# Row maxima of the attention scores as sixteen more rows of the query stack

## What is computed

```python
def reference(x, w_qkv, b_qkv, w_out, b_out, w12, w3, gate_w):
    xn = _layernorm(x, axis=-1)
    return x + attention(xn, ...) + experts(xn, ...)

# attention: 16 heads of 16 features, windows of 128 tokens every 64 tokens
    scores = jnp.einsum('bhnqd,bhnkd->bhnqk', qw, kw) / jnp.sqrt(jnp.float32(D))
    probs = jax.nn.softmax(scores, axis=-1)
    ow = jnp.einsum('bhnqk,bhnkd->bhnqd', probs, vw)
# experts: the best 2 of 8 for each token, softmax of their gate scores as weights
    h12 = jnp.einsum('btd,ehd->bteh', x, w12)
    hidden = jax.nn.silu(h1) * h2
    expert_out = jnp.einsum('bteh,edh->bted', hidden, w3)
```

## Time and profile before

| what | value |
|---|---|
| median of 3 runs | 773.25 us (772.63 to 775.06) |
| the profiled execution | 772.46 us |
| its span in the profile | 770.3 us |
| PE busy | 709.6 us (92%) |
| DVE busy | 579.9 us (75%) |
| ACT busy | 416.8 us (54%) |
| POOL busy | 318.0 us (41%) |

### The profile page before, as it was taken

One profiled execution on the slowest core, in us unless ns is written; L12 is line 12 of the kernel. 1 busy time (PEld: TensorE's weight loads), 2 busy tenths in 40 slices (PEclk: granted clock), 3 DMA queues, 4 the chain that ended last, 5 costly groups with the idle time before them and its releaser, 6 DMA issues.

```text
span 770.3 us, 18229 instructions
## 1 busy us (share of the span) xinstructions
PE 709.6 (92%) x6144; PEld 570.6 (74%) x6145; DVE 579.9 (75%) x975; ACT 416.8 (54%) x769; POOL 318.0 (41%) x360
## 2 busy tenths in 40 slices
PE   0997788797999999999999999999989999999995
PEld 0986566685888778887888778878868787877784
DVE  4953897976787777777777777778758869797884
ACT  0221133235667667676676676766734555655653
POOL 4000369211435445444454444444411235566653
PEclk9975799998999999999999999999999999999999
DMA  8898083472111111111111111111136677875830
GB/s 280 303 327 231 27 221 117 116 240 89 49 48 48 48 54 48 48 49 52 49 51 44 53 49 48 54 44 49 49 101 192 199 230 203 253 206 174 220 116 29
DMA packets 66179, 92.61 MB, mean 120 GB/s; under 512 B 6257, under 2 KB 53233, under 8 KB 66129
## 3 DMA queue, kind: packets, MB, share of 16 engines
q1 hardware_dynamic: 56096, 65.68, 28.5%
q0 software_dynamic: 6864, 18.75, 7.7%
q10 hardware_dynamic: 3168, 7.48, 2.8%
HBM read 59.06 MB, written 32.83 MB: 119 GB/s over the span
## 4 chain that ended last, share of the span: by engine, by line
PE 79%; DVE 11%; DMA 3%; issue 3%; ACT 2%; POOL 1%; SPq 1%; DVEq 0%; ACTq 0%; POOLq 0%
PE PS L1143 71%; PE PS L1370 4%; DVE SMALL L839 3%; DVE XN L1010 2%; PE PS L1348 2%; DMA XN<-in_x 2%; PE PS L1166 1%; DVE WALL L833 1%; PE PS L1226 1%; DMA xt_scratch<-WALL 1%; POOL XN L575 1%; ACT WORK L673 1%; DVE WORK L912 1%; SPq L371 1%; DVE WORK L919 0%
## 5 line engine op out<-in xcount | busy, mean ns | idle before, releaser
L333 DVE TENSOR_TENSOR WS<-WALL,WS 128x1024 fp32r<-128x1024 f32 x144 | 176.5, 1226 | 86.8 <-ACT WS L765 82.8
L1143 PE MATMUL PS<-WS,XTS 128*128 128x512 f32 x852 | 234.3, 411 | 2.1 <-DVE XTS L833 1.6
L1143 PEld LDWEIGHTS PS<-WS,XTS 128*128 128x128 f32 x852 | 151.0, 190 | 46.3 <-DVE XTS L833 13.3
L765 ACT ACTIVATE WS<-WALL 128x1024 fp32r x144 | 152.2, 1058 | 38.3 <-issue 35.8
L1143 PE MATMUL PS<-WALL,WORK 128*128 x568 | 136.3, 383 | 0.8 <-ACT WORK L781 0.8
L1143 PEld LDWEIGHTS PS<-WALL,WORK 128*128 128x128 f32 x568 | 102.2, 190 | 13.1 <-issue 1.0
L616 POOL DMA_INDIRECT WORK<-xn_scratch,WORK x72 | 98.3, 1366 | 23.8 <-issue 21.6
L707 ACT ACTIVATE WORK<-PS 128x512 f32<-128x512 f32 x128 | 69.8, 595 | 63.9 <-PE PS L1143 61.1
L620 POOL DMA_INDIRECT ys_scratch<-SIDE,WORK x36 | 41.6, 1156 | 115.5 <-ACT SIDE L791 115.5
L583 POOL TENSOR_TENSOR OTS<-SIDE,XN 128x256 f32<-128x256 f32 x32 | 23.8, 745 | 147.6 <-DVE XN L1010 99.6
L839 DVE TENSOR_REDUCE SMALL<-PS 128x8 f32<-128x1024 f32 x64 | 77.7, 1214 | 8.9 <-PE PS L1143 8.9
(11 more groups left out here) (125 smaller groups left out, 1082.6 us busy)
## 6 DMA issues: line engine op xcount, KB each, us to landing
WALL<-ys_scratch SPq DMA_DIRECT2D x16, 512.0 KB, 6.8
parts_scratch<-WORK SPq DMA_DIRECT2D x32, 240.0 KB, 2.6
QS<-parts_scratch SPq DMA_DIRECT2D x16, 480.0 KB, 4.4
WALL<-in_wexp ACTq DMA_DIRECT2D x16, 384.0 KB
WALL<-in_wexp SPq DMA_DIRECT2D x16, 384.0 KB
XN<-in_x SPq DMA_DIRECT2D x4, 1024.0 KB, 12.8
xn_scratch<-XN SPq DMA_DIRECT2D x4, 1024.0 KB, 6.9
WALL<-in_x SPq DMA_DIRECT2D x8, 512.0 KB, 5.7
```

Source lines behind the costliest of these rows:

```text
L333: eng.tensor_tensor(out=WS[:, 1 - k, half, 1], in0=weights, in1=WS[:, 1 - k, half, 0].bitcast(F32), op=ALU.subtract).then_inc(low_ready[ha ...
L765: act.activation(WS[:, 1 - k, half, 0], weights, ACT.Copy).then_inc(high_ready[half], 1)
L1143: return pe.matmul(o, a, b, start=start, stop=stop)
```

## The change

The negated maxima are no longer added by a matmul of their own. `KS` gets 16 more rows (`DEEP` = 112). They are constant: in row `96 + 8 * part + i` stand ones for every head whose number modulo 8 is `i`, and zeros elsewhere. `QS`'s buffer already has 128 partitions; its rows 96 to 111 now get the negated maxima, for all eight heads of the unit side by side, on the window's 128 columns. One matmul over 112 rows then gives the shifted scores. The copy out of `T_BANK` moves from DVE (`take_negm`, 16 x 128 elements) to ACT (`take_shift`, line 711 of the changed file, 16 x 1024 elements), where it is the first instruction of a step, ahead of `take_part` or `take_values`. `SEL` and `NEGM` go. `EJ` gets a buffer of its own, with the same readers. `CONSTS` falls from 22 to 18 (one fill and two selects of `SEL`, one fill of `NEGM`), and POOL makes the constant rows behind them: one fill and two selects over 16 x 10240 bf16 elements. PE waits for these before its first `scores`.

```diff
@@ -61,6 +61,7 @@
 STK = NLEV * HD
+DEEP = STK + 2 * HH
 BLOCKS = (0, 2, 1, 3)
@@ -119,8 +120,8 @@
         QS = QALL[0:STK]
-        EJ = QALL[STK:STK + 1, 0, 0, 0:2 * XS_TILES].bitcast(I32)
-        KS = sb("KS", [STK, 2, H, SPAN], BF16)
+        KS = sb("KS", [DEEP, 2, H, SPAN], BF16)
+        EJ = sb("EJ", [1, XS_TILES], I32)[:]
 
@@ -130,14 +131,12 @@
         IDB = IDF[:].bitcast(BF16).rearrange("p (n k) -> p n k", k=2)[:, :, 1]
-        SEL = sb("SEL", [STK, HH, P], BF16)
         SIDE = sb("SIDE", [P, D])
...
         UNIT = sb("UNIT", [P, 3 * HD])
-        NEGM = sb("NEGM", [STK, 2, P], BF16)
         PW = sb("PW", [P, 2, NT])
@@ -246,6 +245,7 @@
 
+        SHIFT_ROW = T_BANK[STK:DEEP, 0:P // 2].bitcast(BF16)
         TOK_BANK = (bank(5), bank(6))
@@ -319,7 +319,7 @@
 
-        CONSTS = 22
+        CONSTS = 18
 
@@ -505,10 +505,6 @@
                                    pattern=[[-1, P]], channel_multiplier=1))
-            one(pool.memset(SEL[:], 0.0))
-            for part in range(2):
-                one(pool.affine_select(out=SEL[:], in_=SEL[:], compare_op=ALU.not_equal, fill=1.0, base=-HH * part,
-                                       pattern=[[-1, HH], [0, P]], channel_multiplier=1))
             one(pool.memset(ONES, 1.0))
@@ -516,7 +512,6 @@
             one(pool.memset(UNIT[:, HD:2 * HD], 0.0))
-            one(pool.memset(NEGM[:], 0.0))
             one(pool.memset(ONE8, 1.0))
@@ -535,6 +530,12 @@
             assert made == CONSTS, made
+
+            rows = KS[STK:DEEP].rearrange("p a (g h) t -> p (a g) h t", h=HH)
+            one(pool.memset(rows, 0.0))
+            for part in range(2):
+                one(pool.affine_select(out=rows, in_=rows, compare_op=ALU.not_equal, fill=1.0, base=-HH * part,
+                                       pattern=[[0, 4], [-1, HH], [0, SPAN]], channel_multiplier=1))
 
@@ -702,6 +703,14 @@
 
+            def take_shift(par, u):
+
+                n, half = u // 2, u % 2
+                to = QALL[STK:DEEP, par, half * HH:(half + 1) * HH, n * STRIDE:n * STRIDE + WIN]
+                act.wait_ge(t_full, c["T"].add())
+                act.activation(to, SHIFT_ROW.unsqueeze(1).to_broadcast([2 * HH, HH, WIN]), ACT.Copy
+                               ).then_inc(t_free, 1)
+
             def exps(u, q):
@@ -728,6 +737,8 @@
                 for u in range(UNITS):
+                    if not (last and u == UNITS - 1) and not (b == EXTRA and u == 0):
+                        take_shift((b + (u + 1) // UNITS) % 2, (u + 1) % UNITS)
                     if not last and u < 4:
@@ -747,12 +758,14 @@
                         exps((u + 1) % UNITS, 1)
+            take_shift(0, 0)
             exps(0, 0)
...
                         batch(b)
+                    take_shift(EXTRA % 2, 1)
                 else:
@@ -979,14 +992,8 @@
 
-            def take_negm():
-                k = c["T"].now() % 2
-                dve.wait_ge(t_full, c["T"].add())
-                dve.tensor_copy(NEGM[0:2 * HH, k, :], T_BANK[0:2 * HH, 0:P // 2].bitcast(BF16)).then_inc(t_free, 1)
-
             take_max()
             take_max()
-            take_negm()
             take_max()
@@ -1058,8 +1065,6 @@
                 for u in range(UNITS):
-                    if not (last and u == UNITS - 1) and not (b == EXTRA and u == 0):
-                        take_negm()
                     if b == EXTRA and u == 0:
@@ -1087,8 +1092,6 @@
                     c["W"].add(NWIN)
-                if b == EXTRA - 1:
-                    take_negm()
                 if ends(b):
@@ -1215,7 +1218,7 @@
                     last = mm(S_BANKS[:, h * WIN:(h + 1) * WIN], QS[:, par, half * HH + h, w],
-                              KS[:, par, half * HH + h, w])
+                              KS[0:STK, par, half * HH + h, w])
                 last.then_inc(s_full, 1)
@@ -1223,7 +1226,7 @@
                 wait_some(pe, t_free, g)
-                pe.transpose(T_BANK[0:2 * HH, 0:P // 2].bitcast(BF16), MH[:, g % 2, :], IDB).then_inc(t_full, 1)
+                pe.transpose(SHIFT_ROW, MH[:, g % 2, :], IDB).then_inc(t_full, 1)
                 c["T"].add()
@@ -1236,8 +1239,7 @@
                         o = ST_BANK[q][:, hq * WIN:(hq + 1) * WIN]
-                        mm(o, KS[:, par, half * HH + h, w], QS[:, par, half * HH + h, w], True, False)
-                        last = mm(o, SEL[:, h, :], NEGM[:, u % 2, :], False, True)
+                        last = mm(o, KS[:, par, half * HH + h, w], QALL[0:DEEP, par, half * HH + h, w])
                     last.then_inc(st_full, 1)
@@ -1273,6 +1275,7 @@
             pe.wait_ge(values_taken, NWIN)
+            pe.wait_ge(consts_made, CONSTS + 3)
             scores(0, 0)
```

## The result

The changed kernel is slower, by little but clear of the noise. Its median is 784.17 us (782.8 to 784.29, 4 runs), against 774.15 us (772.63 to 776.82, 4 runs) for the kernel before on the same chip: a ratio of 1.0122, with a 95% interval of 1.0089 to 1.0154. I had predicted 757.0 us, with a range of 751 to 765.5. The profiled execution took 784.09 us with a span of 782.1 us, 11.8 us more than before.

The account below looks back on a forecast made before the run. In the attention stretches PE was taken to bound steps 4 to 7 and DVE steps 0 to 3. The sum 772.46 - 12.8 - 4.2 + 0.8 = 756.3 us, adjusted to the median, gave 757.0 us, range 751 to 765.5.

Parts of the forecast that it names:

- The constants: Start of the kernel: POOL's fill and selects slow some twenty small DVE instructions by 0 to 0.11 us each; 0.8 us lost.
- The sign that I had named: Start of the kernel: a first turning of tiles later by over 1 us would show the prediction wrong.
- The 38 us of cover: Between POOL's constants, done at 39.5 us, and the first scores at 78.00: time that hides making the constants.
- The statistics as evidence: Start of the kernel: POOL's iotas beside the first statistics cost these nothing, so 0.8 us lost was taken, not 2.
- The products in steps 4 to 7: Batches 4 to 6: four product groups of 0.44 us plus 0.7 us gained, together 2.4 us; 2.0 us after `take_part`'s delay.
- The copies off DVE: Batches 4 to 6, DVE's run to the reciprocal's end: two copies of 0.13 us fewer, 0.3 us earlier.
- ACT: New shift copy: 0.95 to 1.06 us each, 61 us in all, mostly in ACT's waits; 28.8 us of ACT a batch.
- Sequences 0 and 1: First attention stretch: 4.2 us gained in sum, from fewer PE products and DVE copies and an earlier routing map.
- The last stretch in all: Attention from 565 us to the end: 2.6 + 2.5 + 6.0 + 1.7 = 12.8 us gained.
- the rival of the clock: Steps 0 to 3 of five batches: PE idles more, its clock falls, up to 10 us each; 790 and more; chance 0.03.
- ACT as a bound: Batches 4 to 6: at 2.06 us a copy ACT takes 37.7 us a batch; slower, 781 us; chance 0.05.
- Nothing is won: Whole kernel: start and steps cancel, by late constants or a late copy; 773 us; chance 0.04.

## Why the prediction was wrong, step by step

- **The constants: the step that failed.** I took 0.8 us of loss at the start, with 2.2 as the upper bound; it was 17.8 us. The sign that I had named, a first turning later by over 1 us, came true. The durations of POOL's instructions were sized rather high (9.5 and 11.6 us each against 8.63 and 9.03), and the place was right: beside the first statistics. What failed was the price of overlap. I bounded it by rows in which POOL's neighbours were all short, 0.17 against 0.28 us for a cast, and no such row can show a wait that lasts until POOL's instruction ends, when that instruction is 9 us long. Some twenty instructions of 0.11 us each was the wrong form of sum; the right one was: as many holds as there are long POOL instructions, each up to the instruction's whole length, here three holds of 3.7, 8.7 and 6.0 us, 18.4 together (the load of x came 0.5 us earlier, hence 17.8).
- **The 38 us of cover** for the first scores was right for what waits for the constants (even in pieces, POOL is done at 62 us, the first scores come at 83), and beside the point: the loss went through DVE, which doesn't wait for them. "A cover" must be asked for the engine beside, too.
- **The statistics as evidence.** I argued that POOL's iotas beside the first statistics cost these nothing. That is true even of fills and selects (2.71 us for eight, with and without them). But the instructions behind the statistics have other forms, and those were held.
- **The products in steps 4 to 7.** I took 4 x 0.44 + 0.7 = 2.4 us a batch; measured alone they are worth 1.05, and a batch of the changed kernel got 0.97 us shorter where my sum had 2.0. The price of a product was about right (PE's busy time in a batch fell by 2.88 us with 64 fewer), and so was 112 rows at the price of 96 (0.62 us for eight of either), but I let DVE's run end at step 3. With PE faster, DVE's maxima set the pace to step 5, and only the interval of steps 5 to 7 gets shorter, by 0.7 to 0.9 us. I had read the earlier trace rows, in which the chain is PE alone from 650.07 on, as a stretch in which PE is the only bound. DVE stood right behind it. The version with less work on DVE bears this out: it sets another 1.7 us free.
- **The copies off DVE.** I took 0.3 us of DVE's run for two of them. In a batch 1.4 us of copies went and DVE's busy time fell by 0.35, since some of its small instructions got longer; why is not shown.
- **ACT.** Copy: 1.016 us, inside my 0.95 to 1.06. Batches 4 to 6: 29.2 us of ACT, I had 28.8. There it cost little. But the overlap of 0.1 us at each end of a copy did not come: from the start of the exponentials to the start of `scale` it was 0.97 us in the last batch before (745.96 to 746.93) and is 2.15 now (750.19 to 752.34), 1.18 for a copy that I had at 0.95. In the last batch I left ACT out of the sum and forecast 1.5 us of gain: 0.1 came. Copying as words brings 6 us in all, 3.5 of them in the last stretch.
- **Sequences 0 and 1**: 4.2 us predicted, 3.1 from the first scores to the first expert matmul. The mean granted clock of this stretch fell from 0.91 to 0.87, a term that my sum didn't have; what it cost is not shown. With ACT making the rows the same stretch gives 1.0 us, with the copy as words too 3.4.
- **The last stretch in all**: 12.8 us predicted, 4.2 measured. The granted clock was 1.00 from its start to its last `sides`, so the rival of the clock, which had it fall in every batch, did not come; only the last projection ran at the 1.2 GHz level and lost 0.9 us. No rival of mine gave "slower" for the reason that made it so. ACT as a bound was the nearest in name only, and "Nothing is won" had late constants in it, but at 773 us.

With 0.8 replaced by 17.8 and 12.8 by 4.2, the sum is 772.46 - 4.2 - 4.2 + 17.8 = 781.9 us, and with 3.1 for the first sequences 783.0, against the 784.09 of the profiled execution; the 0.7 and 0.5 us ahead of the first scores and in the experts' loop make up the rest.

## What to carry to other kernels

Before a long GpSimd instruction is laid beside VectorE work, ask what each VectorE instruction there is held by, for the whole length of the long one, even if nobody waits for its result: cut it up, give it to another engine, or put it where VectorE waits anyway. A chain that shows one engine alone does not say how far the next one stands behind; with both cut the gain comes, as the version with the constant rows by ACT, the copy as words and the maxima in one row shows: 0.9782 of the time of before (0.9751 to 0.9814), and 0.967 of the changed kernel by the medians (758.31 / 784.17, not run beside each other). When a copy on ScalarE moves bf16 pairs unchanged, move them as 32-bit words: 0.589 us for 1.016.

## What the runs showed of the hardware

A GpSimd instruction can hold a VectorE instruction until it ends, and the form of both decides. Beside a fill of 8.6 us TENSOR_SCALAR was held (3.86, 7.08, 8.62 us in place of 0.17); TENSOR_TENSOR and SCALAR_TENSOR_TENSOR were not, unless they stood behind a held TENSOR_SCALAR. Beside a select of 9.0 us, which also reads SBUF, SCALAR_TENSOR_TENSOR (8.83 us) and TENSOR_TENSOR (6.38 us for three) were held. BATCH_NORM_STATS2 was held by neither. The Trainium skill (SBUF — State Buffer, SBUF: two separate sides) says just this: the pair of ports that VectorE and GpSimd share is an exclusive lock, taken "for the whole instruction", by VectorE instructions in a 2-port mode against any GpSimd instruction, and by those with two SBUF inputs only against one that reads SBUF. This case's traces agree in each row above; that the TENSOR_SCALAR runs in a 2-port mode here no trace shows. My prediction had weighed only that the two engines contend, and priced a lock as if it were a share of bandwidth.

The last projection ran at either clock level after the same 3.10 us in which PE had no work: 1.13 us at the upper one, in the kernel before, and 2.07 at the lower one, in the changed kernel. Two profiled executions can differ by 0.9 us through this alone.

What stays open: why the first sequences gave 3.1 us and not 4.2, with how much of it due to the lower granted clock, and why they gave only 1.0 us when ACT made the constant rows.
